# A recurrent loop on four engines: the kept part of the state moves to GpSimd, and one candidate scan moves ahead of a low half on VectorE

## What is computed

```python
def step(hprev, gxt):                     # gxt: this position's input, already multiplied
    gh = hprev @ whh.T + bhh
    r = sigmoid(gxt[:, :h] + gh[:, :h])               # reset
    z = sigmoid(gxt[:, h:2*h] + gh[:, h:2*h])         # keep
    n = tanh(gxt[:, 2*h:] + r * gh[:, 2*h:])          # candidate
    return (1.0 - z) * n + z * hprev
```

## Time and profile before

| what | value |
|---|---|
| time, median of three runs | 1262.82 us (1260.11 to 1264.99) |
| profiled execution: its own time | 1265.31 us |
| profiled execution: span from first to last instruction | 1263.5 us |
| stretch of the loop in L2 (311 to 748 us): TensorE busy, VectorE busy, ScalarE busy | 430.6, 342.2, 275.8 us of 437 |
| stretch of the loop in L3 (803 to 1240 us): the same | 430.3, 342.2, 276.0 us of 437 |
| GpSimd busy in both stretches | 0 us |
| granted TensorE clock in the two stretches | 0.50 and 0.51 of full speed |

### The profile page before, as it was taken

How to read it: one execution, slowest core, us unless ns; L and a number is a source line. 1 busy time by engine, 2 the same in 40 slices (tenths; PEclk the granted TensorE clock), 3 DMA queues, 4 the chain that set the end, 5 groups by cost and what they waited for, 6 DMA issues and landing times. The chain is left out here.

```text
span 1263.5 us, 60733 instructions
## 1 busy us (share of the span) xinstructions
PE 1142.3 (90%) x24696; PEld 991.4 (78%) x24696; DVE 943.2 (75%) x5715; ACT 670.5 (53%) x4263; POOL 129.8 (10%) x100
## 2 busy tenths in 40 slices
PE   3778799748999999999999967999999999999995
PEld 2545254344999999999999964799999999999985
DVE  4553799964777777777777785677777777777776
ACT  4223601016666666666666652666666666666663
POOL 1001299740000000000000002000000000000000
PEclk8587799957555555555555555755555555555555
DMA  4000000000000000000000000000000000000000
GB/s 115 2 12 1 31 28 27 27 19 1 5 4 4 4 4 4 4 4 4 4 4 4 5 2 7 3 4 4 4 4 4 4 4 5 4 4 4 4 4 26
DMA packets 7955, 12.94 MB, mean 10 GB/s; under 512 B 5649, under 2 KB 6833, under 8 KB 7384
## 3 DMA queue, kind: packets, MB, share of 16 engines
q1 hardware_dynamic: 7674, 9.06, 2.3%
HBM read 8.27 MB, written 0.79 MB: 7 GB/s over the span
## 5 line engine op out<-in xcount | busy, mean ns | idle before, releaser
L1107 PE MATMUL L3s_early<-L3s_h_hi,L_w_hidden 97*128 97x8 f16 x4096 | 200.2, 175 | 4.9 <-DVE L3s_h_hi L1019 4.0
L1107 PE MATMUL L2s_early<-L2s_h_hi,L_w_hidden 97*128 97x8 f16 x4096 | 200.2, 176 | 4.8 <-DVE L2s_h_hi L1019 4.1
L1107 PEld LDWEIGHTS L3s_early<-L3s_h_hi,L_w_hidden 97*128 97x128 f16 x4096 | 163.7, 109 | 26.2 <-DVE L3s_h_hi L1019 7.8
L1107 PEld LDWEIGHTS L2s_early<-L2s_h_hi,L_w_hidden 97*128 97x128 f16 x4096 | 163.7, 109 | 25.9 <-DVE L2s_h_hi L1019 7.4
L1019 DVE TENSOR_TENSOR_SCAN L3s_h_hi<-L3s_renew,L3s_terms 96x32 f16<-96x32 f32 x512 | 113.2, 221 | 85.2 <-ACT L3s_terms L1059 59.4
L1019 DVE TENSOR_TENSOR_SCAN L2s_h_hi<-L2s_renew,L2s_terms 96x32 f16<-96x32 f32 x512 | 113.1, 221 | 85.2 <-ACT L2s_terms L1059 59.4
L1059 ACT ACTIVATE L2s_terms<-L2s_cand 96x16 f32<-96x16 f32 x512 | 111.7, 218 | 93.8 <-DVE L2s_cand L1004 62.4
L1059 ACT ACTIVATE L3s_terms<-L3s_cand 96x16 f32<-96x16 f32 x512 | 111.7, 218 | 93.7 <-DVE L3s_cand L1004 62.7
L1053 ACT ACTIVATE L2s_reset<-L2s_early 96x16 f32<-96x16 f32 x512 | 92.6, 181 | 68.3 <-PE L2s_early L1107 62.7
L1053 ACT ACTIVATE L3s_reset<-L3s_early 96x16 f32<-96x16 f32 x512 | 92.6, 181 | 68.2 <-PE L3s_early L1107 62.6
L1107 PE MATMUL L3s_early<-L3s_h_lo,L_w_hidden 96*128 96x8 f16 x2048 | 127.3, 171 | 0.1
(11 more groups left out here) (229 smaller groups left out, 2884.5 us busy)
## 6 DMA issues: line engine op xcount, KB each, us to landing
L_w_input_raw<-in_L_wih SPq DMA_DIRECT2D x2, 1164.0 KB
l_w_raw<-in_L_w SPq DMA_DIRECT2D x1, 1296.0 KB
L_w_hidden_raw<-in_L_whh SPq DMA_DIRECT2D x2, 582.0 KB
stream<-in_x SPq DMA_DIRECT2D x2, 384.0 KB, 3.6
out<-stream SPq DMA_DIRECT2D x4, 192.0 KB, 2.1
l_idft<-in_idft SPq DMA_DIRECT2D x1, 400.0 KB
rpe_lw<-in_rpe_lw SPq DMA_DIRECT2D x1, 384.0 KB
l_dft<-in_dft SPq DMA_DIRECT2D x1, 288.0 KB, 3.0
```

The costliest lines, as they stand in the source:

```text
L1107: return e.matmul(dst, weights.hidden[0:rows, wp, GATES * (2 * g + j) + gate, :], rhs, start=False, stop=False, skip_group_check=True)
```

## The change

The kept part is taken out of VectorE's program and becomes a program of its own on GpSimd, with a semaphore `kept_ready` of its own, for which `new_state` waits. The kept part of group g in step q waits on GpSimd for `keep` (the semaphore `activated`) and for the state of the step before (`updated`). On VectorE the candidate scan of group 1 now stands ahead of `rest` of group 0. The counts of `updated` follow from this. The diff, without its unchanged parts:

```diff
+        kept_ready = each("kept_ready")
...
-                for s, n in ((updated[1], 2), (hi_ready[0], 1), (hi_ready[1], 1), (lo_ready[0], 1)):
-                    e.sem_inc(s, n)
-
-                BEFORE = (0, 2)
+                for s in (hi_ready[0], hi_ready[1], lo_ready[0]):
+                    e.sem_inc(s, 1)
...
-                def kept_part(g, q):
-
-                    x = q % 2
-                    e.wait_ge(activated[g], 3 * q + 2)
-                    e.tensor_tensor(terms[g][:, x, :, 1], keep[g][:, x], states[g][:, q, :, 1], ALU.mult)\
-                        .then_inc(updated[g], 1)
-
                 def new_state(g, q):
 
                     x = q % 2
                     e.wait_ge(activated[g], 3 * q + 3)
-                    e.wait_ge(updated[g], 2 * q + 1 + BEFORE[g])
+                    e.wait_ge(kept_ready[g], q + 1)
...
                 def rest(g, q):
 
-                    e.wait_ge(updated[g], 2 * q + 2 + BEFORE[g])
+                    if q >= 0:
+                        e.wait_ge(updated[g], q + 1)
...
                 for q in range(SEQ):
                     candidate(0, q)
                     rest(1, q - 1)
-                    kept_part(0, q)
                     new_state(0, q)
+                    candidate(1, q)
                     rest(0, q)
-                    candidate(1, q)
-                    kept_part(1, q)
                     new_state(1, q)
-                e.wait_ge(updated[1], 2 * SEQ + BEFORE[1])
+                e.wait_ge(updated[1], SEQ)
+
+            @block.gpsimd
+            def _(e):
+
+                for q in range(SEQ):
+                    x = q % 2
+                    for g in range(GROUPS):
+                        e.wait_ge(activated[g], 3 * q + 2)
+                        if q > 0:
+                            e.wait_ge(updated[g], q)
+                        e.tensor_tensor(terms[g][:, x, :, 1], keep[g][:, x], states[g][:, q, :, 1], ALU.mult)\
+                            .then_inc(kept_ready[g], 1)
```

## The result

The changed kernel took 1297.91 us in the median of 4 runs (1295.62 to 1299.41), the kernel before 1261.46 us beside it (1259.8 to 1264.99): a ratio of 1.0278, 95% interval 1.0262 to 1.0295. It is slower by 36 us, where 26 were forecast. The profiled execution took 1295.62 us, its span is 1293.8 us. TensorE's granted clock in the two loops is 0.50 of full speed (1.2 GHz, the lower of its two levels), where it was 0.50 and 0.51 before, so the clock is not what changed.

A forecast was written before the change was run, and what follows sets the result against it. VectorE's written order with ScalarE's two tanh was taken to bound the kernel at 1.69 us a step. The change was to give 1.74, and 512 x 0.05 = 26 us more made 1289 on the median, range 1247 to 1350.

The forecast's parts named there:

- Ring A: VectorE's written order with ScalarE's two tanh: sets the old pace, 1.69 us a step; 1.48 after the change.
- Ring C: Both groups, reset to candidate to other group's rest to low products to its reset: 0.81, twice a step 1.62.
- Ring D: TensorE's queue, where other products stand behind low products waiting for rest: 1.62 or 1.78 in turn, mean 1.70.
- 0 to +5 us for the new order: Candidate scan of group 1 ahead of group 0's rest on VectorE: by itself should give nothing, 1.70 us a step.
- The kept product on GpSimd: Takes 0.27 us; path from reset's start 0.70 against 0.71 through tanh, so it fits with nothing left.
- The 0.08 for the hand-over to GpSimd: Time from keep's end to the start of GpSimd's product, about 0.08 us, one term of the 0.70 path.
- The meeting with rest: GpSimd's product and VectorE's rest collide reading SBUF: middle of 1.70 and 1.78 taken, 1.74 us a step.
- The price of 0.076: Delay in us of a VectorE two-input instruction for one meeting with a small GpSimd instruction, 0.946 against 0.870.
- Nothing measurable: Rival: GpSimd's product is shorter than 0.27 and reads in a gap; 0 to +5 us, 1263 to 1268; chance 0.18.
- The faster case: Rival: ring D doesn't bind, no collision, ring C sets 1.62 to 1.66; 1247, at best 1227; chance 0.12.
- The long hold: Rival: GpSimd's product holds rest its whole length, 0.27 twice a step; 1503, half hold 1365; chance 0.13.
- The slow product: Rival: GpSimd's product takes 0.47, 1.80 us a step; 1319, with the collision about 1345; chance 0.15.

The follow-up runs named there:

- order-alone run: Kernel before with group 1's candidate scan ahead of group 0's low half, kept product still on VectorE: 1298.35 us, ratio 1.0264 to the kernel before.
- run without inputs: Changed kernel without the input products of chunks 2 to 31 (output not the layer's): 1276.75 us in one run.
- run with spread ones: Changed kernel with input products reordered to 6 reset, 3 candidate, 6 keep, 3 candidate: 1274.2 us, ratio 1.0078 to the kernel before.
- second experiment: Changed kernel with group 0's low half back ahead of group 1's candidate scan, kept product on GpSimd: 1261.62 us, ratio 0.9967 to the kernel before.

## Why the prediction was right, and where it was off

- **Ring A goes, and gives nothing.** Right. The low half's wait left VectorE's ring, whose length would have been 1.48, and the step became longer, as another ring took over. Shown by the order-alone run, which has the whole loss.
- **Ring C, 0.81 a half step.** The mechanism was right and the size too small: 0.86. Candidate to rest took 0.14, not 0.12, and low products to reset 0.31, not 0.28. Both of my terms came from places where the instruction stood in a queue behind another and was fed at once; where the engine had been idle for it, the same pair is longer. The earlier trace rows had the 0.14 (803.34 to 803.48), in the first step, and I took the other row.
- **Ring D, 1.62 and 1.78 in turn, mean 1.70.** Right in kind, shown twice, by the run without inputs and the run with spread ones, each 0.05 us a step faster. It measured 1.82 in the heavy step, 0.04 more: 0.02 at candidate to rest, 0.01 at low products to reset (0.29) and 0.01 for the low products themselves (0.18). And I took the mean of its two lengths where the light step is set by ring C (1.72): the order alone is worth 1.77, not 1.70. This is the step of the sum that failed: it said 0 to +5 us for the new order, and it was +33 (1298.35 against 1265.02 beside it).
- **The kept product on GpSimd, 0.27, with no room.** It took 0.254, and in the second experiment mostly 0.21. The 0.08 for the hand-over to GpSimd was read between two of GpSimd's own instructions, which is no hand-over; that keep's end to the product's start is 0.08 too (1021.49 + 0.17 to 1021.74) was luck. The room is as small as worked out: doubled, it costs 25 us. In its place it costs nothing.
- **The meeting with rest, 0.04 a step.** Wrong: 0 in the changed kernel. The starts fall together, as said, but GpSimd's begins 0.02 ahead and neither delays rest (0.146, as in the run without it) nor h. It is the product that gives way: 0.254 here against 0.214 in the second experiment, where most low halves lie elsewhere. The price of 0.076 was what VectorE paid where GpSimd paid most, as the last section shows. The term that I left out and the one that I put in nearly cancelled, so that 1289 is near 1298 for a reason that is half wrong.
- **The rivals.** "Nothing measurable" had the right idea on the meeting and the wrong one on ring D. The faster case fell on ring C itself, which alone is slower than ring A. The long hold is real as a mechanism, with a long product; this product is too short and too well placed for it. The slow product is out: 0.254, not 0.47.

## What to carry to other kernels

When an instruction is moved ahead of another on an in-order engine, follow the one that is now behind: here it released a second engine whose answer the moved instruction itself waits for, and so two groups that had been independent were tied into one ring. Take hand-over times from rows in which the receiving engine was idle, if it will be idle for it; 0.02 to 0.03 us at each of four hand-overs made the light steps here 0.10 us longer (1.72 for 1.62), some 25 us over 256 of them. And where two rings take turns, add the longer of them step by step, not the mean of one. Before a long wait in one row is given a cause, look at the same place in a kernel that lacks this cause.

## What the runs showed of the hardware

- VectorE's two-input instruction is held until a two-input product of GpSimd beside it is done: 499 of 512 scans end 0.08 behind the end of a product of 0.45 us, and a low half of 0.15 that started 0.02 behind such a product took 0.46. A memset of 0.46 in the same place delays nothing.
- The 0.076 of a meeting in the earlier trace rows is VectorE's share alone. GpSimd's instruction there was longer than where VectorE ran none with two inputs: 1.23 us in the mean (165 to 234 us) against 0.62 (136.6 to 149 us), in the trace of the kernel before.

```profile
L671 POOL TENSOR_SCALAR l_diag<-ident,l_coef_parts 96x128 f16<-96x128 f32 x58 | 70.5, 1233 | 0.0
L671 POOL TENSOR_SCALAR l_diag<-ident,l_coef_parts 96x128 f16<-96x128 f32 x8 | 4.8, 618 | 0.1
```

- With both starting within 0.03 us, the one that pays differs: in the changed kernel GpSimd (0.254 against 0.214), in the old order with GpSimd one low half in four (0.22 against 0.17). In both GpSimd's product has the earlier start by 0.02 to 0.03, so the order of the starts doesn't decide it, and what does is not shown.
- The unloaded hand-over is longer than the loaded one on TensorE: low products to reset 0.31 where TensorE had waited for the low half (1021.96 to 1022.27), 0.29 where it had not (1023.80 to 1024.09).
- Two GpSimd products of 96x16 follow each other at 0.18 us, less than the 0.22 that each one lasts; where the first lasts 0.25 or 0.26, at 0.22.
- The kernel before has eight high-half scans in L3 that start 0.38 to 0.40 behind tanh's end, 32 steps apart, where 0.03 is usual; the changed kernel has four, 64 steps apart. No run shows why.
